# Opening of a transformer block rearranged: partner queries by a second matmul, weight preparation moved to POOL, the second token group later

## What is computed

```python
h = _layernorm(x) * (1 + ca) + sa
q = einsum('bti,oi->bto', h, Wq)   # 8 heads of 64; k likewise, v: 8 heads of 128
q = _rotary(q, Tx, D)              # x * cos + rot(x) * sin, rot swaps the halves of a head and negates one
...
scores = einsum('bhtd,bhsd->bhts', q, k) * D ** (-0.5) * decay
o = einsum('bhts,bhsv->bhtv', scores, v)
mean, var = ...                    # of o over a head's 128 values
o = (o - mean) * rsqrt(var + EPS)
```

## Time and profile before

| | before |
|---|---|
| time, median of 3 runs | 756.68 us (756.54 to 758.75) |
| span of the profiled execution | 754.3 us |
| PE busy | 737.0 us (98%) |
| DVE busy | 605.7 us (80%) |
| POOL busy | 586.0 us (78%) |
| ACT busy | 489.5 us (65%) |

### The profile page before, as it was taken

One profiled execution on the slowest core, in us unless ns is written; L12 is line 12 of the kernel. 1 busy time (PEld: TensorE's weight loads), 2 busy tenths in 40 slices (PEclk: granted clock), 3 DMA queues, 4 the chain that ended last, 5 costly groups with the idle time before them and its releaser, 6 DMA issues.

```text
span 754.3 us, 29013 instructions
## 1 busy us (share of the span) xinstructions
PE 737.0 (98%) x12148; PEld 647.7 (86%) x12148; DVE 605.7 (80%) x1273; ACT 489.5 (65%) x953; POOL 586.0 (78%) x641
## 2 busy tenths in 40 slices
PE   6999999999999999999999999999999999999987
PEld 5778888888889888988988988888898888888875
DVE  6987787979788787988879798797878878786555
ACT  3576657666675766767566676766666575656664
POOL 2778788888789887898878888788878987776751
PEclk9999999999999999999999999999999999999999
DMA  9320000001011010111102001110101101010000
GB/s 328 102 38 17 16 17 17 16 17 29 10 30 38 9 45 16 24 37 30 31 10 50 17 23 31 27 33 17 44 13 27 38 13 26 16 24 19 22 14 29
DMA packets 56161, 25.67 MB, mean 34 GB/s; under 512 B 36184, under 2 KB 53856, under 8 KB 56032
## 3 DMA queue, kind: packets, MB, share of 16 engines
q1 hardware_dynamic: 55312, 23.02, 12.8%
q10 hardware_dynamic: 720, 0.80, 0.3%
HBM read 11.22 MB, written 4.20 MB: 20 GB/s over the span
## 4 chain that ended last, share of the span: by engine, by line
PE 91%; POOL 2%; issue 2%; DVE 2%; ACT 2%; DMA 0%; POOLq 0%; DVEq 0%
PE ring L309 52%; PE outs L309 15%; PE O_E L309 13%; PE ring L324 8%; PE O_O L309 2%; PE ring L354 2%; POOL qT L1306 0%; POOL gn_rstd L1322 0%; POOL ln_rstd L1278 0%; DMA X<-in_x 0%; ACT y L744 0%; POOL y L1329 0%; ACT y L797 0%; DVE delta L1074 0%; POOL X L1343 0%
## 5 line engine op out<-in xcount | busy, mean ns | idle before, releaser
L1329 POOL TENSOR_TENSOR y<-y,gate 128x512 f32<-128x512 f32 x123 | 158.5, 1304 | 35.7 <-ACT y L744 35.7
L706 ACT ACTIVATE v<-ring 64x512 f32<-64x512 f32 x128 | 76.0, 594 | 81.5 <-PE ring L309 80.7
L309 PEld LDWEIGHTS outs<-wo_gated,y 128*128 128x128 f32 x992 | 119.7, 192 | 6.5 <-POOL y L1329 1.9
L1312 POOL TENSOR_TENSOR rot_k<-rot_k,sin_k 128x256 f32<-128x256 f32 x128 | 106.2, 849 | 24.6 <-DVE sin_k L1025 24.6
L309 PE MATMUL outs<-wo_gated,y 128*128 128x128 f32 x992 | 121.8, 275 | 1.1 <-POOL y L1329 1.0
L1052 DVE TENSOR_REDUCE gn_sum<-N 128x4 f32<-128x512 f32 x118 | 75.5, 681 | 42.4 <-ACT N L732 42.4
L1322 POOL TENSOR_TENSOR gn_rstd<-gn_var,minus_half 128x8 f32<-128x8 f32 x64 | 105.3, 1645 | 5.0
L1306 POOL TENSOR_TENSOR qT<-qT,swapped 128x512 f32<-128x512 f32 x64 | 82.8, 1293 | 28.9 <-DVE swapped L1008 28.9
L1032 DVE TENSOR_TENSOR A<-ring,consts 128x256 f32<-128x256 f32 x128 | 47.9, 414 | 60.0 <-PE ring L309 60.0
L744 ACT ACTIVATE y<-ring,gn 128x512 f32<-128x512 f32 x126 | 90.8, 776 | 5.1 <-PE ring L324 5.1
L714 ACT ACTIVATE kT<-ring 128x512 f32<-128x512 f32 x64 | 38.2, 597 | 77.8 <-PE ring L324 77.8
(11 more groups left out here) (173 smaller groups left out, 2089.4 us busy)
## 6 DMA issues: line engine op xcount, KB each, us to landing
k_odd<-rot_k SPq DMA_DIRECT2D x128, 64.0 KB, 2.4
X<-in_x SPq DMA_DIRECT2D x16, 256.0 KB, 3.7
out<-X SPq DMA_DIRECT2D x15, 256.0 KB, 2.5
key_tables<-in_const SPq DMA_DIRECT2D x7, 256.0 KB, 8.2
rotary_q<-in_const_q SPq DMA_DIRECT2D x2, 512.0 KB, 8.2
...
```

Source lines behind the costliest of these rows:

```text
L309: return e.matmul(o, lhsT, rhs, start=start, stop=stop, skip_group_check=True)
L706: done = e.activation(v[halves(half), i % 2, 1, :, :], by(PAIRS, bank_of["v", odd, i][halves(1 - half), :]), ACT.Copy)
L1312: done = e.tensor_tensor(turned[:, n, :, :], turned[:, n, :, :], sin[:, n, :, :], op)
L1329: e.tensor_tensor(y[:, n % NY, :], y[:, n % NY, :], gate[:, n % 2, :], ALU.mult).then_inc(sem["y"])
```

## The change

Group 0's queries are rotated without a shuffle. A second set of query weights, in which the 16-column blocks are exchanged by pairs (`w_partners`, kept in the `mix_k` buffers, which are free until later), gives the partners' projection directly into another PSUM bank (`O_E` or `O_O`); DVE multiplies it by the sine table, and POOL subtracts. Splitting the query and key weights and centring the value weights move from DVE to POOL; scaling the mean moves to ACT; the value weights are prepared in two halves. DVE applies group 0's norm in place of ACT. Group 1's statistics, norm, transposition and queries move to later places of all four lists, and group 2's statistics too. The three fillers go from 12 narrow, 15 wide and 7 wide matmuls to 6 narrow and 3 wide. `square(i)` for the first four chunks waits for one weight each and not for three. The loop behind the opening is the same, and so is SP's list.

```diff
+            def project_q_pair(p):
+
+                cols = slice(p * P, (p + 1) * P)
+                bank = take_bank(("q", p), ("cos_q", p + 1))
+                at.wait_ge("w_qk_lo", 1)
+                at.wait_ge("hT_hi", 1)
+                at.wait_ge("hT_lo", 1)
+                split_matmul(bank[:, :], [wqk[s][:, cols] for s in ("hi", "lo")], h_parts(0))
+                at.wait_ge("w_partners_lo", 1)
+                at.wait_ge("sin_q", p - 1)
+                bank = bank_of["q_partners", p] = O[p % 2][:, :, :].rearrange("p n v -> p (n v)")
+                split_matmul(bank, [mix_k[s][:, cols] for s in ("hi", "lo")], h_parts(0)).then_inc(sem["proj_q"])
...
-                at.wait_ge("w_v_lo", 1)
+                at.wait_ge("w_v_lo", 1 if odd else 2)
...
+                at.wait_ge("sin_q", PAIRS)
...
-            keep_busy(out_bank, 12, False)
-            project_q(0)
-            project_q(1)
-            project_q(2)
-            project_q(3)
+            keep_busy(out_bank, 6, False)
+            project_q_pair(0)
             project_k(0)
+            project_q_pair(1)
+            project_q_pair(2)
             project_v(0, 1)
-            keep_busy(out_bank, 15, True)
+            project_q_pair(3)
             project_v(0, 0)
-            transpose_n(1, 0)
             project_k(1)
-            keep_busy(out_bank, 7, True)
             transpose_k(0)
             project_v(1, 1)
+            keep_busy(out_bank, 3, True)
             scores(0)
             state(0)
-            project_q(4)
             mod_gates()
             project_v(1, 0)
             project_k(2)
...
-            project_q(5)
+            transpose_n(1, 0)
...
-            project_q(6)
+            project_q(4)
             project_v(3, 1)
+            project_q(5)
             project_v(3, 0)
             project_k(4)
             free_heads(1)
...
+            project_q(6)
+            project_v(4, 1)
             project_q(7)
-            project_v(4, 1)
             project_v(4, 0)
             project_k(5)
             transpose_n(2, 0)
...
+            def scale_v_mean():
+                at.wait_ge("v_sum", 1)
+                e.activation(v_mean[:, :], v_mean[:, :], ACT.Copy, scale=1.0 / V).then_inc(sem["v_mean"])
+
+            def round_w_v(odd):
+                cols = slice(odd * W, (odd + 1) * W)
+                at.wait_ge("w_v_centred", 1 if odd else 2)
+                e.activation(wv["hi"][:, cols], raw_vc[:, cols], ACT.Copy).then_inc(sem["w_v_hi"])
...
+            def round_w_partners():
+                at.wait_ge("w_qk", 16)
+                e.activation(with_partners(mix_k["hi"][:, :]), with_partners(raw_qk[:, 0:H * D])[:, :, ::-1, :], ACT.Copy
+                             ).then_inc(sem["w_partners_hi"])
...
-            norm_apply(0, 0)
+            round_w_partners()
             round_h(0)
-            split_w_v()
-            norm_apply(1, 0)
+            scale_v_mean()
+            round_w_v(1)
+            round_w_v(0)
+            split_w_g()
             copy_v(0, 1)
+            copy_kT(0)
             copy_v(0, 0)
-            round_h(1)
-            copy_kT(0)
-            split_w_g()
             copy_v(1, 1)
             copy_v(1, 0)
             copy_kT(1)
-            round_w_k()
+            norm_apply(1, 0)
             square(0, 0)
             square(0, 1)
+            round_h(1)
             copy_v(2, 1)
             copy_v(2, 0)
             copy_kT(2)
+            round_w_k()
             scale_norm()
...
+            def first_apply():
+                at.wait_ge("ln_shift0", 1)
+                for j in range(GC):
+                    e.tensor_scalar(normed[:, j, :], X[:, 0, j, :], ln_rstd[:, 0, j:j + 1], ln_shift[:, 0, j:j + 1],
+                                    ALU.mult, ALU.add).then_inc(sem["ln_apply0"])
...
+            def rotate_q_pair(p):
+
+                at.wait_ge("const_q0", 16)
+                at.wait_ge("proj_q", p + 1)
+                at.wait_ge("qT", p - 1)
+                e.tensor_tensor((turned, swapped)[p % 2][:, :], bank_of["q_partners", p], rotary_q[:, 1, 0:W], ALU.mult
+                                ).then_inc(sem["sin_q"])
+                e.tensor_tensor(qT[:, 0, p, :], bank_of["q", p][:, :], rotary_q[:, 0, 0:W], ALU.mult).then_inc(sem["cos_q"])
...
             norm_stats(0, 0)
-            split_w("w_qk", raw_qk, wqk)
+            first_apply()
             mod_columns()
             full_h(0)
+            low_h(0)
             sum_w_v()
-            low_h(0)
-            centre_w_v()
+            rotate_q_pair(0)
+            rotate_k(0)
+            low_w_v(1)
+            rotate_q_pair(1)
+            low_w_v(0)
+            rotate_q_pair(2)
+            rotate_q_pair(3)
+            rotate_k(1)
             norm_stats(1, 0)
-            rotate_q(0)
-            split_w("w_v", raw_vc, wv)
-            rotate_q(1)
-            rotate_q(2)
-            rotate_k(0)
-            rotate_q(3)
-            full_h(1)
-            rotate_k(1)
-            norm_stats(2, 0)
             mask(0, 1)
             mask(0, 0)
             add_state(0)
             mod_gates()
-            rotate_q(4)
             rotate_k(2)
             mask(1, 1)
             mask(1, 0)
             add_state(1)
-            rotate_q(5)
+            full_h(1)
             rotate_k(3)
             norm_heads(0, 0)
             mask(2, 1)
             mask(2, 0)
             norm_heads(0, 1)
             add_state(2)
-            rotate_q(6)
+            rotate_q(4)
+            norm_stats(2, 0)
+            rotate_q(5)
             rotate_k(4)
             norm_heads(1, 0)
             mask(3, 1)
             norm_heads(1, 1)
             mask(3, 0)
             add_state(3)
+            rotate_q(6)
             rotate_q(7)
             full_h(2)
...
+            def low_w_partners():
+                at.wait_ge("w_partners_hi", 1)
+                e.tensor_tensor(with_partners(mix_k["lo"][:, :]), with_partners(raw_qk[:, 0:H * D])[:, :, ::-1, :],
+                                with_partners(mix_k["hi"][:, :]).bitcast(F32), ALU.subtract).then_inc(sem["w_partners_lo"])
+
+            def centre_w_v(odd):
+
+                cols, heads = slice(odd * W, (odd + 1) * W), slice(odd * PAIRS, (odd + 1) * PAIRS)
+                at.wait_ge("v_mean", 1)
+                e.tensor_tensor(by(PAIRS, raw_vc[:, cols]), by(PAIRS, raw_v[:, cols]),
+                                v_mean[:, heads].unsqueeze(2).broadcast_to([P, PAIRS, V]), ALU.subtract).then_inc(sem["w_v_centred"])
...
+                if g == 0:
+                    at.wait_ge("cos_q", m + 1)
+                    at.wait_ge("sin_q", m + 1)
+                    e.tensor_tensor(q, q, (turned, swapped)[m % 2][:, :], ALU.subtract).then_inc(sem["qT"])
+                else:
+                    at.wait_ge("swapped", m - PAIRS + 1)
+                    e.tensor_tensor(q, q, swapped[:, :], ALU.add).then_inc(sem["qT"])
...
             norm_rstd(0, 0)
+            split_w_qk()
+            low_w_partners()
+            centre_w_v(1)
+            centre_w_v(0)
             rotate_q(0)
-            norm_rstd(1, 0)
+            rotate_k(0)
             rotate_q(1)
             rotate_q(2)
-            rotate_k(0)
             rotate_q(3)
-            low_h(1)
             rotate_k(1)
+            norm_rstd(1, 0)
             split_w_g()
-            rotate_q(4)
             rotate_k(2)
             head_rstd(0)
+            low_h(1)
             rotate_k(3)
+            rotate_q(4)
+            head_rstd(1)
             norm_rstd(2, 0)
             rotate_q(5)
-            head_rstd(1)
-            rotate_q(6)
             rotate_k(4)
             head_rstd(2)
             gate_weights(0, 0)
+            rotate_q(6)
             rotate_q(7)
             low_h(2)```

On POOL, from the end of group 0's norm (`ln_shift`), the list before began with the query additions and group 1's norm:

```order
L1281 TENSOR_TENSOR ln_shift<-ln_neg,ln_rstd 128x4 [waits ln_rstd0]
L1306 TENSOR_TENSOR qT<-qT,swapped 128x512 [waits swapped]
L1274 TENSOR_TENSOR ln_var<-ln_mv,eps 128x4 [waits ln_apply0,ln_mv0]
L1276 TENSOR_SCALAR ln_neg<-ln_mv 128x4
L1278 TENSOR_TENSOR ln_rstd<-ln_var,minus_half 128x4 [waits ln_var0]
L1281 TENSOR_TENSOR ln_shift<-ln_neg,ln_rstd 128x4 [waits ln_rstd0]
L1306 TENSOR_TENSOR qT<-qT,swapped 128x512 [waits swapped] x2
L1312 TENSOR_TENSOR rot_k<-rot_k,sin_k 128x16x16 [waits sin_k]
```

38 lines of the change are left out of this document (16 added, 22 removed).

## The result

| | before | after |
|---|---|---|
| time, median (lowest to highest) | 756.61 (756.53 to 758.75), 4 runs | 761.82 (761.21 to 764.57), 4 runs |
| ratio, 95% interval | | 1.0071 [1.0053, 1.0089] |
| span of the profiled execution | 754.3 | 759.8 |
| first scores | 27.89 | 24.48 |
| marker (key transposition of chunk 5) | 64.25 | 69.26 |

A forecast was written before the change was run, and what follows sets the result against it. PE was taken to bound the kernel, carrying changes at the opening's end through. -3.65 at first scores, +1.8 moved DVE work, +2.85 shuffle wait, +1.0 ACT copies and PE waits gave +2.0: 758.7 us, range 753.4 to 760.8.

The forecast's parts named there:

- the likeliest case: Before the marker, a loop through POOL, ACT and DVE closes late: +0.3 to +3.5 us, taken as +2.0; chance 0.44.
- the landing of the moved keys: At state of chunk 0: keys land at about 24.3, ahead of need at 24.8, hidden by 0.5 us only.
- the chain ahead of ACT's copies of chunk 2: Group 1's h_full ends at 33.4, ACT's copies of chunk 2's values at 35.7, scores of chunk 2 at 36.7.
- PE's clock behind the loop's own wait: No cost forecast there; a fall to 1.2 GHz was considered only between 16 and 24 us.
- Query 0 at 11.75, first scores at 24.25: In the opening: query 0 at 11.75 against 13.46, first scores at 24.25 against 27.89, 3.65 us gained.
- Rival (3): At the start, POOL's split holds the port against DVE's norm instructions; all the rest moves: +3.2, 759.9 us; chance 0.10.
- Scores of chunk 1 at 29.2, of chunk 2 at 36.7: Behind the first scores: the schedule's times for these scores, with 4.4 us kept chunk for chunk until query 4's rotation.
- ACT waits 3.5, the shuffle 2.85: ACT idles about 3.5 us ahead of group 2's norm; DVE's shuffle of query 7 loses 2.85 us waiting for POOL.
- Query 8 at 60.8, marker at 66.0 to 66.6: End of the opening: query 8 waits for the mask until 60.8; marker at 66.0 to 66.6 against 64.25.
- From the marker to the end: From the loop on, PE sets the pace, so a delay or gain at the marker carries to the last instruction.
- rival (4): PE's clock falls between 16 and 24 us, +3, 761.7 with (1), or moved keys land late, costing 1; chance 0.08.
- (1): The likeliest case: the loop through POOL, ACT and DVE closes late before the marker, +2.0 us; chance 0.44.

The follow-up runs named there:

- e2_apply_first: The changed kernel with POOL's split of the query and key weights waiting until DVE has applied group 0's norm: 761.84 us, ratio 1.0068 to the kernel before.
- e5_apply_keys: e2_apply_first with SP's move of chunk 0's keys issued ahead of its last loads: 760.64 us, ratio 1.0055 to the kernel before.
- c4_round_late: c2 with ACT's copies of v(2) put ahead of its rounding of group 1's h: 755.49 us, ratio 0.9989 to the kernel before.
- c2: c1 with SP's move of chunk 0's keys issued ahead of its last loads: 757.52 us, ratio 1.0011 to the kernel before.
- e3_fill_scores4: The changed kernel with nine zero-adding narrow matmuls between attend and recall of chunk 3: 760.92 us, ratio 1.0059 to the kernel before.
- e6_apply_fill: e2_apply_first with nine zero-adding narrow matmuls ahead of recall of chunk 3: 759.95 us, ratio 1.0050 to the kernel before.
- e1: The changed kernel with group 2's statistics on DVE and norm on POOL moved ahead of query 4: 758.96 us, ratio 1.0032 to the kernel before.
- c1: The changed kernel with the edits of e1 and e2_apply_first together: 757.99 us, ratio 1.0027 to the kernel before.
- p1: The changed kernel with group 1's norm, transposition, h and queries and group 2's statistics and norm back in their earlier places: 760.90 us, ratio 1.0059 to the kernel before.

## Why the prediction was too low

The direction that the likeliest case gave was right, and so was its mechanism, the loop through POOL, ACT and DVE; the size of the sum was not. Three steps of it failed, and each had been put too low: the landing of the moved keys (put at nothing, "hidden by 0.5 us only"; it took 0.9), the chain ahead of ACT's copies of chunk 2 (0.6 more than the schedule had), and PE's clock behind the loop's own wait (put at nothing; it took 1.0). Step by step:

- **Query 0 at 11.75, first scores at 24.25.** Measured 12.76 and 24.48. Rival (3) occurred: the port was held at the start. Its price of +3.2 did not come, since "all the rest moves" was wrong: the exchange of DVE and POOL had slack, the first scores moved by 0.2, and with this contention taken away (e2_apply_first) the time stayed. The Trainium skill's rule (SBUF — State Buffer, "Who interferes with whom"), that the pair of ports is held for the whole instruction, agrees with this trace: an instruction of DVE that starts beside POOL's ends with it, 3.15 or 4.12 us for four against 1.11.
- **The keys, "hidden by 0.5 us only".** Measured: `state(0)` at 25.80 and not 24.8. This is the first mis-sized term: 0 was in the sum, and of the 1.0 us here 0.6 are the wait for the keys. I had counted the issue of SP's loads and the full DMA engines, but took the keys to land as soon as the engines come free; SP came to them at 19.78, the second of their two transfers was issued at 20.5 and took 5.2 us to land (2.2 to 2.5 before, where no loads stood ahead), and `state(0)` had them 6 us after 19.78. From the first key transposition to the second e5_apply_keys takes 5.67 us, e2_apply_first 6.61 and after 6.52, so the keys cost 0.9 us in the profiles; by the times of e5 it is 1.0 to 1.2, not clear of noise. I had given it 0.08 together with the clock.
- **Scores of chunk 1 at 29.2, of chunk 2 at 36.7.** Measured 30.33 and 38.47. Of the 1.1 at chunk 1, 0.9 are the keys and 0.2 the later first scores. Another 0.6 appeared on the way to chunk 2, in the chain `add_state`, `h_full(1)`, ACT's copies, `attend(1)`; I had this chain in the schedule, but not as a cost of its own. c4_round_late shows that it was one: with it cut, chunk 2 takes 1.3 us less, and with the clock drop that followed in c2 1.7 to 2.0 us of time come back.
- **ACT waits 3.5, the shuffle 2.85.** Measured 3.38 and 2.81. The loop is right in place and in size. From the rotation of query 4 (42.4 predicted, 42.89 + 0.68 and a shuffle to 44.2 measured) on everything lies 1.7 to 1.9 us late by the terms above: the shuffle ends at 58.1 (56.4), the scores of chunk 4 come at 60.22 (58.5).
- **Query 8 at 60.8, marker at 66.0 to 66.6.** Measured 62.47 and 69.26, 6.8 us and not 5.5 apart. The second mis-sized term: behind its wait of 2.09 PE ran partly at 1.2 GHz. e3_fill_scores4 and e6_apply_fill both give 1.0 for it in the profile, from the scores of chunk 4 to the marker. I had looked for a lower clock only between 16 and 24 us, where the change takes fillers away, and not behind the wait that my own loop made.
- **From the marker to the end** nothing was gained or lost beyond 0.5 us, as assumed.

The sum was +2.0; with +1.7 up to chunk 2 (0.2 of it the late first scores), +1.0 for the clock and 0.3 left over it is the +5.0 at the marker. That rival (4) with (1) had come to 761.7, next to the 761.8 measured, is luck: its 3 us were a lower clock between 16 and 24 us, where it stayed at 1.00. These terms are not independent: the start, the keys and the clock were small or unclear when tried alone on after, since another wait stood behind each. With the edits added in order the medians fall steadily (761.8, 759.0, 758.0, 757.5, 755.5), but only the first step, the loop, and the last, ACT's rounding, are clear of the intervals.

What stays open: the worth in time of the free start once the loop is open (1.2 us at the marker in the profiles of e1 and c1, with overlapping intervals of the times) and of the earlier keys, and how much of p1's loss is the clock.
